# A software pipeline for two pair layers: a lag of its own for every stage, chunks loaded ahead, and work moved between VectorE, GpSimd and ScalarE

## What is computed

```python
# layer 0
z_norm = layer_norm(z) * ln_w + ln_b
a = (z_norm @ W_ap + b_ap) * sigmoid(z_norm @ W_ag + b_ag) * mask
b = (z_norm @ W_bp + b_bp) * sigmoid(z_norm @ W_bg + b_bg) * mask
out = einsum('bikc,bkjc->bijc', a, b)
x = z + (out @ W_z + b_z)
# layer 1
x = layernorm(pair_repr) * ln1_w + ln1_b
left  = sigmoid(x @ left1)  * (x @ left2)
right = sigmoid(x @ right1) * (x @ right2)
p = layernorm(einsum('nsre,nkre->nske', left, right)) * ln2_w + ln2_b
g = sigmoid(x @ gate)
return residual + (p @ out_w) * g
```

## Time and profile before

| | us |
|---|---|
| median of 3 runs | 1250.62 (1250.57 to 1250.93) |
| the profiled execution | 1251.89 |
| its span, first to last instruction | 1250.1 |
| PE, DVE, ACT, POOL busy | 896.1, 837.5, 580.1, 526.6 |

### The profile page before, as it was taken

One profiled execution on the slowest core, in us unless ns is written; L12 is line 12 of the kernel. 1 busy time (PEld: TensorE's weight loads), 2 busy tenths in 40 slices (PEclk: granted clock), 3 DMA queues, 4 the chain that ended last, 5 costly groups with the idle time before them and its releaser, 6 DMA issues.

```text
span 1250.1 us, 26342 instructions
## 1 busy us (share of the span) xinstructions
PE 896.1 (72%) x9820; PEld 839.1 (67%) x9820; DVE 837.5 (67%) x1907; ACT 580.1 (46%) x834; POOL 526.6 (42%) x361
## 2 busy tenths in 40 slices
PE   2544444444657787988886888889888988866875
PEld 1434443443557786987875888889888988856864
DVE  4666666666367699499939447771895499089197
ACT  1545455454428465456425445663553454233232
POOL 2323445445546232033126314330674376077177
PEclk9865555565789999999879999999999999989989
DMA  2233323555758886288576625776685387866156
GB/s 77 74 102 101 93 77 115 173 176 160 236 177 272 272 252 192 93 247 275 180 260 187 193 80 175 220 252 221 215 284 178 98 272 239 268 203 204 35 186 202
DMA packets 173237, 228.71 MB, mean 183 GB/s; under 512 B 11064, under 2 KB 109624, under 8 KB 171064
## 3 DMA queue, kind: packets, MB, share of 16 engines
q1 hardware_dynamic: 173112, 227.04, 57.9%
HBM read 134.73 MB, written 92.27 MB: 182 GB/s over the span
## 4 chain that ended last, share of the span: by engine, by line
PE 30%; DVE 27%; issue 16%; ACT 14%; POOL 6%; DMA 5%; SPq 2%; DVEq 0%; ACTq 0%; POOLq 0%
PE bank L975 16%; DVE stats L804 7%; ACT xt L624 5%; POOL rstd L549 5%; DVE xc L837 4%; PE ps_w L1005 4%; DVE split L844 4%; DMA chunk<-xt 3%; PE bank L955 3%; ACT sig L600 3%; PE bank L956 2%; ACT chunk L642 2%; DVE lhs L778 2%; DVE xin L817 2%; PE ps_x L1016 2%
## 5 line engine op out<-in xcount | busy, mean ns | idle before, releaser
L549 POOL TENSOR_TENSOR rstd<-var,minus_half 128x8 f32<-128x8 f32 x192 | 328.0, 1709 | 685.5 <-DVE var L812 685.5
L975 PE MATMUL bank<-rhs,lhs 128*128 128x128 f32 x2048 | 242.9, 280 | 23.2 <-POOL lhs L543 10.2
L975 PEld LDWEIGHTS bank<-rhs,lhs 128*128 128x128 f32 x2048 | 238.0, 196 | 24.1 <-issue 19.9
L1016 PE MATMUL ps_x<-ident_b,split 128*128 128x128 bf16 x1024 | 98.2, 253 | 187.6 <-DVE split L844 182.0
L600 ACT ACTIVATE sig<-bank 128x512 f32<-128x512 f32 x256 | 152.7, 597 | 132.1 <-PE bank L956 130.4
L1016 PEld LDWEIGHTS ps_x<-ident_b,split 128*128 128x128 bf16 x1024 | 76.8, 114 | 203.0 <-DVE split L844 176.4
L606 ACT ACTIVATE split<-xc 128x504 bf16<-128x504 f32 x128 | 79.7, 623 | 256.7 <-DVE xc L837 256.7
L955 PE MATMUL bank<-w_rhs,chunk 128*128 128x128 bf16 x1024 | 160.2, 246 | 25.2 <-DVE lhs L778 14.3
L955 PE MATMUL bank<-w_lhs,chunk 128*128 128x128 bf16 x1024 | 156.7, 242 | 28.8 <-DMA chunk<-xt 19.4
L1005 PE MATMUL ps_w<-w_out,opair 128*128 128x128 f32 x1024 | 146.5, 288 | 23.6 <-DVE split L851 20.3
L955 PEld LDWEIGHTS bank<-w_lhs,chunk 128*128 128x128 bf16 x1024 | 138.5, 151 | 35.2 <-DMA chunk<-xt 22.2
(11 more groups left out here) (86 smaller groups left out, 1302.5 us busy)
## 6 DMA issues: line engine op xcount, KB each, us to landing
xt<-xt SPq DMA_DIRECT2D x96, 512.0 KB, 4.3
chunk<-xt SPq DMA_DIRECT2D x80, 512.0 KB, 4.6
xin<-in_x_dram SPq DMA_DIRECT2D x128, 256.0 KB, 3.9
x<-xin SPq DMA_DIRECT2D x64, 256.0 KB, 3.4
xin<-x SPq DMA_DIRECT2D x64, 256.0 KB, 4.1
out_dram<-xin SPq DMA_DIRECT2D x64, 256.0 KB, 3.4
spill<-lhs SPq DMA_DIRECT2D x8, 1024.0 KB, 6.4
chunk<-xcol SPq DMA_DIRECT2D x16, 512.0 KB, 5.0
```

The costliest lines, as they stand in the source:

```text
L549: g.tensor_tensor(rstd[:, m % 2], var[:, m % 2], minus_half[:, :], ALU.pow).then_inc(rooted, 1)
L975: last = mm(bank[:, n], operand["lhs"][:, kh, c, :], operand["rhs"][:, kh, c, :], start=kh == 0, stop=kh == HALVES - 1)
L1016: last = nc.tensor.transpose(ps_x[:, h, n, :], split[:, h, n].rearrange("p a c -> p (a c)"), ident_b[:, :])
```

## The change

- Each kind of tick has a table of lags for all stages (`LAGS`), and each engine's loop asks which step is due for a stage in a tick. The order of stages within an engine's tick is new too.
- z steps: halves are projected 3 ticks after their step. 56 steps begin before the eight ticks with two halves, none in these, and eight within the first contraction (at units 0, 1, 3, 4, 6, 7, 9, 10).
- The centre is on POOL for steps below 22 and from 56 up to 127, on DVE for the others, all p steps among them. Before, it was on DVE for z steps below 52, half of those above and most x steps, and on POOL for half the p steps up to 159.
- POOL's mask in a tick waits for the norm of two steps before, and its root comes last in the tick.
- Masks on DVE are half as large and one per unit (`mask_unit`).
- Six chunks (24 to 29) have buffers of their own in the scratch space of `quad`, and are loaded with 30 and 31 once step 47 is stored. Other chunks are loaded when the buffer comes free.
- `opair` has a second buffer from step 97 to 127, the column stores have four semaphores, the gate's chunk has two buffers in the last two quadrants.
- The spread of the gate's chunk goes from DVE to ACT.
- Layer 0's x steps have mix one tick after turn and add one later; their input is loaded one tick after the step begins (in ticks without chunks in the same one) instead of two before. p steps have stats and root one tick ahead of the tick, norm and turn in it, mix one after.

```diff
+Z_LAGS = dict(load=-2, stats=0, variance=0, root=0, centre=1, norm=1, high=1, low=2, turn_x=2, xt=3,
+              col=3, store=4, project=3, gates=4, make=5)
+X_LAGS = dict(turn=0, turn_out=0, mix=1, load=1, add=2, keep=3, stats=3, variance=3, root=3, centre=4,
+              norm=4, high=4, low=5, turn_x=6, xt=6, store=7, project=0, gates=0, make=1)
+P_LAGS = dict(stats=-1, variance=-1, root=-1, centre=-1, norm=0, turn=0, turn_out=1, mix=1, spread=-2,
+              gate=0, gate_out=2, scale=2, load=2, residual=3, store=4, gate_load=-4, project=0, gates=1, make=1)
+LATE_Z_LAGS = dict(Z_LAGS, turn_x=3, xt=4, col=4, store=5)
...
+    "second half": dict(LATE_Z_LAGS, project=0, gates=0, make=1),
+    "x with chunks": X_LAGS,
+    "x alone": dict(X_LAGS, load=0, add=1, keep=2, stats=2, variance=2, root=2, centre=3, norm=3,
+                    low=4),
+    "x every other tick": dict(X_LAGS, stats=4, variance=4, root=4, centre=5, norm=5, high=5, low=6,
+                               turn_x=7, xt=7, store=8),
+    "p alone": dict(P_LAGS, gate_out=1, spread=-1, gate_load=-4),
+}
...
-    lag = 5
-    for t in range(53):
-        tick(t if t < 52 else None, [t - lag] if t >= lag else [])
+    def tick(phase, m=None, halves=(), unit=None, spill=None):
+        ticks.append((phase, m, tuple(halves), unit, spill))
+    def contraction(q, steps={}, spills={}):
+        for u in range(UNITS):
+            tick("z in contraction", steps.get(u), unit=(q, u), spill=spills.get(u))
...
+    for m in range(3 * STEPS):
+        tick("z", m, [m])
+    for m in range(3 * STEPS, Z_LATE):
+        tick("last z", m)
     for i in range(8):
-        tick(None, [48 + 2 * i, 49 + 2 * i], spill=(0, 0, i // 2) if i % 2 else None)
-    for u in range(UNITS):
-        tick(52 + u if u < 12 else None, unit=(0, u), spill=(0, 1, u // 4) if u % 4 == 3 else None)
+        tick("second half", None, [48 + 2 * i, 49 + 2 * i], spill=(0, 0, i // 2 - 1) if i in (3, 5, 7) else None)
+    contraction(0, dict(zip((0, 1, 3, 4, 6, 7, 9, 10), range(Z_LATE, 4 * STEPS))),
+                {0: (0, 0, 3), 3: (0, 1, 0), 7: (0, 1, 1), 11: (0, 1, 2), 15: (0, 1, 3)})
     for n in range(STEPS):
-        tick(X_BASE + n, [64 + 2 * n, 65 + 2 * n])
-    for u in range(UNITS):
-        tick(unit=(1, u))
+        tick("x with chunks", X_BASE + n, [64 + 2 * n, 65 + 2 * n])
+    contraction(1)
...
+Z_EARLY, Z_LATE = 22, 56
...
+EARLY = range(DIRECT + GROUPS, DIRECT + GROUPS + 6)
...
+def load_tick(n):
+    layer, _, kind, half, group, other = chunk_of(FIRST_OF[n])
+    last = 2 * STEPS + STEPS - 1 if n in EARLY else 0
+    if kind == "row":
+        last = STEPS * (QUADRANTS.index(("z" if layer == 0 else "x", half, other)) + 1) - 1
+    else:
+        last = X_BASE - 1
+    stored = TICK_OF[("store", "step", last)]
+    if n in EARLY:
+        return stored
+    free = TICK_OF[("project", 2 * LAST_OF[ring_before(n)] + 1)]
+    return max(stored, free)
...
-    kind = step(m)[0]
-    quadrant = m // STEPS
-    if kind == "z":
-        return m >= 52 and m % 2 == 0
-    if kind == "x":
-        return quadrant == 7 or (quadrant == 6 and m % 2 == 0)
-    return quadrant < 10 and m % 2 == 0
+    return m < Z_EARLY or Z_LATE <= m < P_BASE
...
+            return opair_2 if PAIRED <= m < P_BASE and m % 2 else opair[:, :, :]
...
+                for m in due("load", t):
+                    if m >= 2:
+                        load_x(m)
+                for m in due("keep", t):
+                    store_x(m)
+                for m in due("store", t, "zx"):
+                    if m % 2:
+                        store_xt(m)
+                    if 2 * STEPS <= m < X_BASE:
+                        store_cols(m)
+                for m in due("store", t, "p"):
+                    store_out(m)
+                for n in LOADS_AT.get(t, []):
+                    load_chunk(n)
...
+                pool.wait_ge(normed, after(m - 1))
...
+                for m in due("centre", t):
+                    if centre_on_pool(m):
+                        centre(m)
+                for m in due("residual", t):
+                    add_residual(m)
                 for n in pool_masks_at(t):
+                    if t < MASK_TWO:
+                        pool.wait_ge(normed, after(t - 2))
                     mask_operand(n)
+                for m in due("root", t):
+                    root(m)
...
+            def spread_gate(m):
+                w = (m - P_BASE) // 2
+                act.wait_ge(gchunk_landed[w % 2], 16 * (w // 2 + 1))
+                act.wait_ge(gate_mm, after(2 * w - 3))
+                if w == 1:
+                    act.wait_ge(mixed, after(4 * STEPS - 1))
+                a.activation(by_vector(gspread[w % 2]), by_group(gchunk_of(w)), ACT.Copy).then_inc(gate_spread, 1)
...
+                for m in due("xt", t):
+                    xt_out(m)
+                for m in due("gate_out", t):
+                    gate_out(m)
+                unit = unit_at(t - 1)
                 if unit and unit[1] % 2:
                     fill_quadrant(GROUPS_C * unit[0] + unit[1] // 2)
+                for m in due("col", t):
+                    col_out(m)
+                for h in due_halves("gates", t):
+                    gates(h)
+                for m in due("high", t):
+                    high(m)
+                for m in due("turn_out", t):
+                    turn_out(m)
+                for m in due("spread", t):
+                    if m % 2 == 0:
+                        spread_gate(m)
...
+                halves = due_halves("make", t)
+                for h in halves[:-1]:
+                    make(h)
+                for m in due("stats", t):
+                    statistics(m)
+                for h in halves[-1:]:
+                    make(h)
+                unit = unit_at(t)
+                if unit and unit[0] in VECTOR_MASKS:
+                    mask_unit(*unit)
+                for m in due("variance", t):
+                    variance(m)
+                for m in due("scale", t):
+                    scale(m)
+                for m in due("norm", t, "p"):
+                    normalise(m)
+                for m in due("centre", t):
+                    if not centre_on_pool(m):
+                        centre(m)
+                for m in due("add", t):
+                    add(m)
+                for m in due("norm", t, "zx"):
+                    normalise(m)
+                for m in due("low", t):
+                    low(m)
...
+                for m in due("turn_x", t):
+                    turn_x(m)
+                for m in due("gate", t):
+                    gate_product(m)
+                if unit_at(t):
+                    contract(*unit_at(t))
+                for h in due_halves("project", t):
+                    project(h)
+                for m in due("turn", t, "x"):
+                    turn(m)
```

More of the change, by code:

```diff
@@ new lines @@
+LATE_Z_LAGS = dict(Z_LAGS, turn_x=3, xt=4, col=4, store=5)
+LAGS = {
+    "z": Z_LAGS,
+    "last z": LATE_Z_LAGS,
+    "z in contraction": LATE_Z_LAGS,
+    "second half": dict(LATE_Z_LAGS, project=0, gates=0, make=1),
[4 more added lines that the diff above has]
+                               turn_x=7, xt=7, store=8),
+    "p with chunks": P_LAGS,
+    "p alone": dict(P_LAGS, gate_out=1, spread=-1, gate_load=-4),
+}
@@ L111, in schedule @@
-    for u in range(UNITS):
-        tick(unit=(3, u))
+        tick("x alone", X_BASE + 2 * STEPS + n)
+    contraction(3)
     for n in range(2 * STEPS):
-        tick(X_BASE + 3 * STEPS + n // 2 if n % 2 == 0 else None, [128 + 2 * n, 129 + 2 * n],
-             spill=(1, 0, (n - 20) // 3) if n in (20, 23, 26, 29) else None)
-    for u in range(UNITS):
-        tick(unit=(4, u), spill=(1, 1, u // 2) if u < 8 and u % 2 == 0 else None)
+        tick("x every other tick", X_BASE + 3 * STEPS + n // 2 if n % 2 == 0 else None,
+             [128 + 2 * n, 129 + 2 * n], spill=(1, 0, (n - 20) // 3) if n in (20, 23, 26, 29) else None)
@@ L118, in schedule @@
+    contraction(4, {}, {2 * n: (1, 1, n) for n in range(4)})
     for n in range(STEPS):
[L119 to L121 removed]
+        tick("p with chunks", P_BASE + n, [192 + 2 * n, 193 + 2 * n])
+    contraction(5)
     for n in range(STEPS):
[L123 to L125 removed]
+        tick("p with chunks", P_BASE + STEPS + n, [224 + 2 * n, 225 + 2 * n])
@@ L145, in halves_at, with due_stages @@
-def halves_at(t):
-    return TICKS[t][1] if 0 <= t < T_END else ()
-def first_half(t):
-    return halves_at(t)[0] if len(halves_at(t)) == 2 else None
-def second_half(t):
-    return halves_at(t)[-1] if halves_at(t) else None
+def due_stages():
+    steps, halves, of_half = {}, {}, {}
+    for t, (phase, m, hs, _, _) in enumerate(TICKS):
+        for stage, lag in LAGS.get(phase, {}).items():
+            if stage in ("project", "gates", "make"):
+                for h in hs:
+                    halves.setdefault((stage, t + lag), []).append(h)
+                    of_half[(stage, h)] = t + lag
```

(11 more changed lines are left out.)

287 lines of the change are left out of this document (86 added, 201 removed).

## The result

The changed kernel takes a median of 1067.57 us (1065.35 to 1071.87, 4 runs), the one before 1250.59 (1249.09 to 1250.93, 4 runs): a ratio of 0.8543, 95% interval 0.8514 to 0.8571. The profiled execution took 1066.57 us with a span of 1064.8, against 1250.1 before, at a mean granted clock of 0.956 against 0.875. Of all executions reported here one is a slow one, the 1096.68 us of the experiment with earlier loads, and the ratio there leaves it out.

What follows compares the result with a forecast made beforehand. It took a loop of ACT and DVE taking turns to bound the early z ticks, mostly DVE or PE later. Segment savings summed to 154.5 us off a 1250.1 span, giving 1096 us; range 1053 to 1149, chance 0.67.

Steps and rivals of the forecast that it cites:

- z ticks: Before the first contraction: ticks of 3.3, then 3.65 us; contraction begins at 257 instead of 359.6, 102 us less.
- the 25 us for the eight ticks: Ticks with two halves before the first contraction: sigmoid, make and projection per bank, 3 us while ACT finishes steps; 25 in all.
- x with chunks: Two x stages: ticks of 4.45 us with DMA near full; 108.7 each against 118.7 and 110.7, 10 and 2 less.
- Layer 1's first operands: PE's 6.37 us per step bounds, waits between banks go; 6.45 a step, 138.7 against 147.3, 8.6 less.
- x alone: x steps without chunks and their contraction: ticks of 3.2 us, 86.5 against 91.5, 5 less.
- p with chunks: Two p stages: spread copy to ACT, all centres to DVE; ticks of 4.4 us, 103.1 against 106.9, 3.8 less, twice.
- p alone: p steps without chunks: ticks of 3.15 us; 85.1 against 92.3 and 61.3 against 67.4, 13.3 less.
- Transfers as the bound: DMA keeps chunk ticks near 4.69 and 4.78, z ticks with columns stretch to 4.4; about 1136 us, chance 0.15.
- DVE and POOL taking turns: POOL's centres and roots exclude DVE's two-input work in z, x and p ticks: 97 us more, about 1190; chance 0.10.
- Slower by the round store, load, add: In x and p steps this round over four xin buffers takes more than about 24 us; 1264 us, chance 0.03.
- A change that does less than its tables say: An overlooked wait keeps z ticks at 5.6 and 5.9 us; about 1190, or 1232 without later gains; chance 0.05.
- rival 2: DVE and POOL exclude each other: z ticks 4.05, later 4.85, x and p alone 4.0; about 1190 us, chance 0.10.

Runs made afterwards that it cites:

- the loop put back: The changed kernel with make moved to the tick of its sigmoid: 1182.88 us, ratio 0.9475.

## Why the prediction was right, and where it was not

The forecast was 1096, the result 1067.57, inside the range. The span came 31 us below the sum, and the segments say where.

- **z ticks: right mechanism, too long.** I had 3.3 and 3.65 and got 3.22 and 3.37 (4.25 and 4.06 for the first two with a mask, 3.88 and 4.20 for two late ones). Below 22 the chain var, root, centre does close on POOL as I had it: 0.17 of waiting, a root of 2.02 with the hand-over, a centre of 1.03. What I hadn't seen is that DVE is full as well (3.21), 0.45 of it being var held by the centre; with the centre off POOL the tick is DVE's own 3.37. From 22 on I added 0.15 to a sum of 3.5 without giving a reason, and the sum is 3.37. With the 25 us for the eight ticks, the 5 us for late inputs (too small, 8.1 measured) and 4 for DMA this made 257 where 247.8 came.
- **x with chunks: 8.8 and 8.4 us too long.** Two steps failed. I held a tick of 4.1 for "hardly to be had" since the DMA share was 0.95 in 4.69 us at 287 GB/s. About the same traffic now ran at a share of 0.99 and 337 GB/s in 3.84: the high busy share was no ceiling on the rate. And I held PE to its 4.12, a modelled busy time; with the same matmuls it is 3.84 in a full tick, so it held time that the work doesn't need. The ticks before the first of these contractions took 63.7 us instead of 76.7, and the contraction itself 36.2 instead of 32: with the longer lags more of the steps' tails run in it, in the first of these the turn_x of five steps where before it was three.
- **Layer 1's first operands: 8.7 too long**, for the same reason: PE's modelled 6.37 a step is 5.95 now that the step is shorter. I should have put the floor below it.
- **x alone** came to 86.5 exactly, but by two misses: ticks of 3.02 for 3.2, a contraction of 34 for 29.5.
- **p with chunks: the number by luck in part.** 104.1 and 103.1 came for 103.1. Undisturbed pairs of ticks do take 8.4 us instead of 9.56, but others take 10.2 (3.86 and 6.33), and from the fourth step on a tick is 4.56 on the mean, not 4.4. The stretch ahead of the contraction takes 74.4 and 73.4 us, where it took 73.1 before: DVE's smaller sum, my reason for the gain, made it no shorter. What is shorter is the contraction, 29.7 instead of 33.8, because two steps' turns, mixes and gate products ran inside it before, and now hardly more than one mix does. My sum had 28.7 there and didn't say why.
- **p alone: 5.4 too short,** or 0.8 to 5.4, as kernels with the same code there took 85.9 to 90.5. I counted DVE and POOL, and not that gate_out on ACT, one tick after its gate, waits for POOL's residual with opair behind it. The edits that put gate_out behind opair in these steps alone agree: the segment then takes 84.2 and 83.5, below the forecast, and the last one 58.9 with ACT's copy in place.
- **PE's wait for masks before the first contraction** is gone as said. In the contraction, PE's longest wait is 2.7 us, for DVE's masks, where POOL had held it 10.22.

**The rivals.** Transfers as the bound (1136): the waits don't show it; the share does reach 0.99 in single ticks, and PE is full in the same ticks. DVE and POOL taking turns (1190): in part, and small; of the changed kernel's 192 norms 9 take over 1 us, of 128 lows 2. Slower by the round store, load, add: not here, but the experiment with earlier loads is that mechanism in another form, SP standing 30.1 us at loads whose buffers are still being stored; one tick more of lag keeps it off in the changed kernel. A change that does less than its tables say: no.

**The rule weighed.** POOL's centre holds DVE's var for 0.45 us, and with no centre beside it var is short. The Trainium skill (SBUF — State Buffer, "Who interferes with whom") says that a DVE instruction with two SBUF inputs and a GpSimd instruction that reads SBUF exclude each other; centre and var agree with it. It also says that a DVE instruction with at most one SBUF input, outside the two-port modes, doesn't contend; the mask on POOL agrees. POOL's timeline in a z tick from 22 on, in the changed kernel:

```profile
130.86 1.95 POOL L627 TENSOR_TENSOR rstd<-var,minus_half 128x8 f32<-128x8 f32 x1 [0.17 <-DVE var L895]
132.77 1.28 POOL L621 TENSOR_TENSOR rhs<-rhs,masks 128x512 f32<-128x512 f32 x1
```

and DVE's:

```profile
130.64 0.67 DVE L912 TENSOR_TENSOR xc<-xin,stats 128x504 f32<-128x504 f32 x1
131.34 0.68 DVE L920 TENSOR_TENSOR xc<-xc,rstd 128x504 f32<-128x504 f32 x1
131.94 0.68 DVE L927 TENSOR_TENSOR split<-xc,split 128x504 bf16<-128x504 f32 x1
132.54 0.88 DVE L887 BATCH_NORM_STATS2 stats<-xin 128x6 f32<-128x128 f32 x4
133.34 0.67 DVE L861 TENSOR_TENSOR rhs<-bank,sig 128x512 f32<-128x512 f32 x1
```

The mask (132.77 to 134.05) lies over statistics and make, each with one SBUF input at most, and costs them nothing. In the eight ticks with two halves, where POOL runs masks one after another, two norms and two lows (two inputs each) took 1.6 to 1.8 us.

The roots are a case of their own, and the one root of the earlier trace rows showed only half of it. A root that starts while a two-input instruction of DVE runs is longer by what is left of that (67 roots of the changed kernel, 1.68 to 2.55 us): started 0.13 us behind the norm (76.77 and 76.64) it takes 2.05 us, 0.22 behind the centre (130.86 and 130.64) 1.95, both times as if it had begun its 1.64 us some 0.53 us after DVE's instruction did. Where none runs as it starts, 116 of 125 roots of the changed kernel take 1.63 to 1.65 us (the other nine 2.07 to 2.10), though up to two of DVE's two-input instructions begin within them, and those keep their 0.68. Before, 34 of 192 roots were longer in the same way (1.94 to 2.07). So DVE can hold a root back, as the rule says, but a root that has started doesn't hold DVE; why isn't shown. Costing roots at nothing for DVE held (for POOL such a start costs 0.3 to 0.4 us, which the 3.3 had allowed for), and rival 2's sum, which made them exclude, did not.

## What to carry to other kernels

If no engine is full in a tick, look for the loop of waits before costing any operation: one line moved behind the normalise gave 109 of 183 us here, and the busy times gave the new tick to 0.1. With the loop open, engines are full, and there it was moved work that counted: 0.60 of the 0.85 us by which an x tick with chunks became shorter is the centre on POOL. Every stage put later in an in-order engine also moves what stands behind it, so follow each edit once round all engines and the DMA queue: the two that looked safest (a copy-out behind opair, a load one tick sooner) each cost over 20 us. A busy share of 0.95 on DMA, and modelled busy times of PE, were no floors of the time here. And a segment read from one execution needs its spread before a gain is put down to an edit.

## What the runs showed that I had not expected

- **The clock.** In the z stage the granted clock was 0.61 before (0.50, or 1.2 GHz, in the ticks of the earlier trace rows), 0.80 with the one moved line, 0.91 in the changed kernel (1.00, or 2.4 GHz, in both ticks shown), and 0.60 with the loop put back. The same work at shorter ticks came with the higher clock; PE's eight turns take 1.04 us in before's tick and 0.62 in the changed one. Neither the loop over ACT and DVE before nor the tick after has PE's work in its bound, so little of the gain should hang on the clock; no run sets it apart.
- **DMA** moved 337 GB/s in an x tick of 3.84 us, where the densest tick shown of before had 287.
- **A root on POOL** that starts 0.13 to 0.23 us behind one of DVE's two-input instructions takes 0.3 to 0.4 us more, and one that is under way doesn't lengthen them; POOL's centre of 128 x 504 does hold such work, down to an add of 128 x 8.
